# Query and key parts laid out feature by feature, with three gathers for each, in a two-layer adaLN transformer kernel

## What is computed

```python
h = layernorm(x) * (1 + ca) + sa                   # sa..gb from silu(c) @ wmod
x = x + ga * attention0(h)                         # linear attention, chunks of 64, RoPE, biases bq bk bv bg
x = x + gb * mlp0(layernorm(x) * (1 + cb) + sb)    # 256 -> 2048 -> 256, weights in 4-bit codes
x = x + ga1 * attention1(...)                      # causal softmax attention, RoPE, biases bq bk
x = x + gb1 * mlp1(...)                            # holds a second causal softmax attention, 1024 hidden
```

## Time and profile before

| | us |
|---|---|
| median of 3 runs | 713.77 |
| lowest and highest run | 713.38, 720.05 |
| the profiled execution's own time | 716.44 |
| its span, first to last instruction | 714.7 |
| mean granted TensorE clock | 0.976 |

### The profile page before, as it was taken

One profiled execution on the slowest core, in us unless ns is written; L12 is line 12 of the kernel. 1 busy time (PEld: TensorE's weight loads), 2 busy tenths in 40 slices (PEclk: granted clock), 3 DMA queues, 4 the chain that ended last, 5 costly groups with the idle time before them and its releaser, 6 DMA issues.

```text
span 714.7 us, 10679 instructions
## 1 busy us (share of the span) xinstructions
PE 651.3 (91%) x3977; PEld 409.9 (57%) x3977; DVE 463.9 (65%) x970; ACT 334.4 (47%) x531; POOL 164.6 (23%) x200
## 2 busy tenths in 40 slices
PE   3699988999999979799999998888999999989996
PEld 3576746777777747444444434574554444368885
DVE  5868776777777388688988801656689887243223
ACT  3335143333333333336567685561555657843332
POOL 6601133555555431210000000030000001002231
PEclk9999599999999999899999999997999999999999
DMA  9502320000000001573000000037420000050001
GB/s 319 164 1 89 89 82 0 23 22 23 1 0 1 0 1 44 182 218 91 3 2 1 2 2 1 0 98 223 134 81 2 2 2 3 1 176 1 0 1 59
DMA packets 36335, 38.35 MB, mean 54 GB/s; under 512 B 3958, under 2 KB 35204, under 8 KB 36028
## 3 DMA queue, kind: packets, MB, share of 16 engines
q1 hardware_dynamic: 36284, 37.68, 16.7%
HBM read 30.13 MB, written 7.34 MB: 52 GB/s over the span
## 4 chain that ended last, share of the span: by engine, by line
PE 47%; issue 22%; POOL 12%; DVE 11%; ACT 3%; DMA 2%; SPq 2%; POOLq 0%; DVEq 0%; ACTq 0%
POOL it_lo L1601 9%; PE psum L777 9%; PE psum L737 8%; PE psum L763 8%; PE psum L452 3%; PE psum L454 3%; PE psum L453 3%; POOL wd L1580 2%; PE psum L495 2%; PE psum L566 2%; SPq L408 2%; PE psum L766 2%; PE psum L740 2%; DVE m L1280 2%; DVE stats L1103 1%
## 5 line engine op out<-in xcount | busy, mean ns | idle before, releaser
L957 ACT ACTIVATE pt<-psum 128x1024 f32<-128x1024 f32 (+1 forms) x192 | 148.0, 811 | 92.9 <-PE psum L766 64.7
L1280 DVE TENSOR_REDUCE mx<-psum 128x1 f32<-128x512 f32 (+3 forms) x216 | 132.4, 665 | 16.3 <-PE psum L737 8.3
L737 PE MATMUL psum<-kr,qr 96*128 96x512 bf16 (+3 forms) x384 | 111.0, 341 | 5.4 <-DMA kr<-parts_scratch 2.5
L1601 POOL TENSOR_TENSOR it_lo<-it,it_hi 128x512 fp32r<-128x512 f32 x48 | 67.3, 1401 | 153.6 <-ACT it_hi L1001 153.6
L763 PE MATMUL psum<-qr,kr 99*128 99x512 bf16 (+3 forms) x384 | 97.6, 327 | 1.5 <-ACT pt L957 1.3
L777 PE MATMUL psum<-pt,vp 128*32 128x512 f32 (+3 forms) x768 | 81.7, 498 | 0.0
L452 PE MATMUL psum<-h_hi,wf_hi 128*128 128x512 f32 x192 | 75.5, 393 | 1.7 <-issue 1.7
L737 PEld LDWEIGHTS psum<-kr,qr 96*128 96x128 bf16 x384 | 37.1, 100 | 67.5 <-DVE mx L1280 29.4
L453 PE MATMUL psum<-h_lo,wf_hi 128*128 128x512 f32 x192 | 75.0, 390 | 0.0
L454 PE MATMUL psum<-h_hi,wf_lo 128*128 128x512 f32 x192 | 74.9, 390 | 0.0
L1001 ACT CAST it_hi<-it 128x512 fp32r<-128x512 f32 x48 | 29.8, 622 | 95.7 <-DVE it L1355 95.7
(11 more groups left out here) (204 smaller groups left out, 1111.2 us busy)
## 6 DMA issues: line engine op xcount, KB each, us to landing
qr<-parts_scratch SPq DMA_DIRECT2D x48, 128.0 KB, 2.7
kr<-parts_scratch SPq DMA_DIRECT2D x48, 128.0 KB, 2.6
parts_scratch<-parts SPq DMA_DIRECT2D x12, 384.0 KB, 3.5
wmod<-in_L_wmod SPq DMA_DIRECT2D x1, 1536.0 KB, 6.1
parts_scratch<-qr SPq DMA_DIRECT2D x4, 384.0 KB, 3.3
x<-in_L_attn_x SPq DMA_DIRECT2D x2, 512.0 KB, 4.0
wmod<-in_L_wmod SPq DMA_DIRECT2D x1, 1024.0 KB, 7.2
packed<-in_L_ffn_gate_W_packed SPq DMA_DIRECT2D x1, 1024.0 KB, 9.2
```

The lines of the kernel that those rows point to most:

```text
L737: m = pe.matmul(b, qr[0:PARTS_ROWS, c, h, (qt - 4 * c) * P:(qt - 4 * c + 1) * P], kr[0:PARTS_ROWS, ch, h, 0:w], start=True, stop=not diag)
L957: act.activation(pt[:, n % 4, :, 0:w], psum[:, b:b + 2, 0:w], ACT.Exp, scale=0.25).then_inc(S["ex"], 1)
L1280: dve.tensor_reduce(dst, bank[at[0]][:, 0:k * w].rearrange("p (k w) -> p k w", k=k), AX, ALU.max).then_inc(S["p1_mx"], 1)
L1601: pool.tensor_tensor(it_lo[:, N % 2, :], it[:, N % 2, :], it_hi[:, N % 2, :].bitcast(F32), ALU.subtract).then_inc(S["it_l"], 1)
```

## The change

- `scr` is laid out [piece, half, part, feature, token]. The columns of the four q and k weight matrices of the second block, and bq and bk of its first attention, are reordered on the way in, so that 16 features x 8 heads follow each other as feature, head; RoPE (`pairs`, `rope_cos`, `rope_sin`) uses views for this order when l = 1 (the first softmax attention; here l counts the block).
- `spread` issues 3 gathers for q and 3 for k, into 48, 32 and 16 neighbouring partitions, each row 8 heads x 512 tokens. For k the source is the first 3, 2, 1 parts, as they lie in scratch. For q it is one part, repeated 3, 2, 1 times by a step of zero. The writes of q and k have semaphores of their own, and the gathers of q wait only for that of q.
- `rest` has four buffers. The overlay of `qr`/`kr` over the mlp's tiles is reordered so that the memset of the -1 rows is split in four behind the last four `it_lo` of mlp(0).
- Biases are loaded once as 12 partitions x 128, split there by POOL in four operations, and brought to 3 partitions x 1536 by three DMAs; SP waits for POOL before it issues these, and issues them ahead of the rest of `wmod0` and what follows. `spin` takes the place of `sel`.
- `idle(14, 0)` is `idle(5, 0)`, `idle(4, 3)` is gone, and ACT computes the Silu ahead of the square root.

```diff
@@ -219,7 +219,7 @@
         y = xn[:, :, :].rearrange("p a b -> p (a b)").rearrange("p (c t) -> p c t", c=KC)
-        rest = xn[:, 0:4, :].rearrange("p a b -> p (a b)").rearrange("p (c t) -> p c t", c=2)
+        rest = xn[:, :, :].rearrange("p a b -> p (a b)").rearrange("p (c t) -> p c t", c=4)
         att = xn
@@ -240,15 +240,16 @@
-        ((packed, wf_hi, wf_lo, wd, nib, sgn, dbl, r16, gl, it, it_hi, it_lo), (_, v1, g, qT, cum, km), (nat,),
+        ((wf_hi, wf_lo, gl, it, it_hi, it_lo, packed, wd, nib, sgn, dbl, r16), (v1, g, qT, km, _, _, cum), (_, nat),
-            [("packed", [P, 3 * F0], I32), ("wf_hi", [P, 2, 6 * P], F32R), ("wf_lo", [P, 2, 6 * P], F32R),
-             ("wd", [P, 2, 6 * P], F32), ("nib", [P, 6 * P], U16), ("sgn", [P, 6 * P], U16),
-             ("dbl", [P, 6 * P], BF16), ("r16", [P, 4 * P], U16), ("gl", [P, 2, HALF], F32),
-             ("it", [P, 2, HALF], F32), ("it_hi", [P, 2, HALF], F32R), ("it_lo", [P, 2, HALF], F32R)],
-            [("packed_", [P, 3 * F0], I32), ("v1", [P, NT, 2, VW], F32), ("g", [P, NT, D], F32),
-             ("qT", [P, KC, T], F32), ("cum", [P, 4, 2, VW], F32), ("km", [P, 2, 2, VW], F32)],
-            [("nat", [P, 3 * F0], F32)],
+            [("wf_hi", [P, 2, 6 * P], F32R), ("wf_lo", [P, 2, 6 * P], F32R), ("gl", [P, 2, HALF], F32),
+             ("it", [P, 2, HALF], F32), ("it_hi", [P, 2, HALF], F32R), ("it_lo", [P, 2, HALF], F32R),
+             ("packed", [P, 3 * F0], I32), ("wd", [P, 2, 6 * P], F32), ("nib", [P, 6 * P], U16),
+             ("sgn", [P, 6 * P], U16), ("dbl", [P, 6 * P], BF16), ("r16", [P, 4 * P], U16)],
+            [("v1", [P, NT, 2, VW], F32), ("g", [P, NT, D], F32), ("qT", [P, KC, T], F32),
+             ("km", [P, 2, 2, VW], F32), ("gap", [P, 7168 - 2 * NT * VW - NT * D - KC * T - 4 * VW], F32),
+             ("packed_", [P, 3 * F0], I32), ("cum", [P, 4, 2, VW], F32)],
+            [("gap2", [P, 7168], F32), ("nat", [P, 3 * F0], F32)],
@@ -269,8 +270,9 @@
-        bias = sb("bias", [P, 6 * D], BF16)
-        sel = sb("sel", [P, P], BF16)
+        brow = sb("brow", [12, P])
+        bpart = sb("bpart", [12, 3, P], BF16)
+        bias = sb("bias", [3, 6 * D], BF16)
@@ -311,22 +313,23 @@
-        scr = nc.dram_tensor("parts_scratch", [4, P, 3, T], BF16, kind="Internal").ap()
+        scr = nc.dram_tensor("parts_scratch", [4, NH, 3, P, HALF], BF16, kind="Internal").ap()
-            idz sel_ok bias_z bias_s bias_ok ident_ok spin_ok const_ok vp_ones kr_ones a_rep_ok b_zero
+            idz bias_s bias_ok ident_ok spin_ok const_ok vp_ones kr_ones a_rep_ok b_zero
+        names += [f"{z}w{i}" for z in "qk" for i in range(4)]
@@ -350,14 +353,16 @@
+            load(brow[:, :], a["bias_rows"].rearrange("(c p) -> c p", p=P), "ld_bias")
             wm0 = a["L0_wmod"].rearrange("(c p) n -> p c n", p=P)
                 load(raw0[:, i], a[f"L0_attn_W{n}"].rearrange("(o p) k -> p o k", p=P), "ld_raw0")
-            sp.wait_ge(S["bias_z"], 1)
-            load(rb[0:P:32, 0:4 * D], a["bias_rows"][0:4 * D].partition_broadcast(4), "ld_bias")
             load(rope_c[:, :, :, :], a["rope_cos"].rearrange("p (l t d) -> p l t d", l=2, t=NT), "ld_rope")
             load(rope_s[:, :, :, :], a["rope_sin"].rearrange("p (l t d) -> p l t d", l=2, t=NT), "ld_rope")
+            sp.wait_ge(S["bias_s"], 4)
+            for i in range(3):
+                load(bias[i:i + 1, :], bpart[:, i, :], "bias_ok")
             load(wmod0[:, :, 512:1536], wm0[:, :, 512:1536], "ld_wmod0b")
@@ -366,8 +371,6 @@
             load(a_nat[:, :, :], a["L1_ffn_A"].rearrange("(o p) r -> p o r", p=P), "ld_a")
-            sp.wait_ge(S["bias_ok"], 1)
-            load(rb[0:P:32, 0:2 * D], a["bias_rows"][4 * D:6 * D].partition_broadcast(4), "ld_bias")
             sp.wait_ge(S["b_zero"], 1)
@@ -394,20 +397,21 @@
                     w2 = 2 * dt + is_k
-                    tok = slice(half * HALF, (half + 1) * HALF)
                     sp.wait_ge(*low_part(l, 4 * half + w2))
-                    sp.dma_start(scr[w2, :, :, tok], piece(l, w2, half)).then_inc(S[f"pw{2 * half + dt}"], 16)
+                    sp.dma_start(scr[w2, half].rearrange("s p t -> p s t"), piece(l, w2, half)).then_inc(S[f"{'qk'[is_k]}w{2 * half + dt}"], 16)
-
-                tok = slice(half * HALF, (half + 1) * HALF)
-                sp.wait_ge(S[f"pw{2 * half + dt}"], 32 * (l + 1))
-                for is_k, (dst, order) in enumerate([(qr, (0, 1, 0, 1, 0, 2)), (kr, (1, 1, 2, 2, 0, 1))]):
-                    for slot, part in enumerate(order):
-                        sp.dma_start(dst[slot:PARTS_ROWS:6, half, 8 * dt:8 * dt + 8, :],
-                                     scr[2 * dt + is_k, :, part, tok].rearrange("(h d) t -> d h t", d=DH)
-                                     ).then_inc(S[f"qr_ld{2 * half + dt}"], 16)
+                for is_k, dst in enumerate((qr, kr)):
+                    sp.wait_ge(S[f"{'qk'[is_k]}w{2 * half + dt}"], 16 * (l + 1))
+                    for part, (first, n) in enumerate(((0, 3), (3, 2), (5, 1))):
+                        src = scr[2 * dt + is_k, half].rearrange("s (d h) t -> s d (h t)", d=DH)
+                        if is_k:
+                            src = src[0:n]
+                        else:
+                            src = src[part:part + 1].to_broadcast([n, DH, 8 * HALF])
+                        sp.dma_start(dst[DH * first:DH * (first + n), half, 8 * dt:8 * dt + 8, :].rearrange("r h t -> r (h t)"),
+                                     src).then_inc(S[f"qr_ld{2 * half + dt}"], 16)
@@ -474,8 +478,10 @@
                 if b0 is not None:
-                    pe.wait_ge(S["bias_ok"], 1 + b0 // T)
-                    m = pe.matmul(dst, sel[:, :], bias[:, b0:b0 + c1 - c0], start=False, stop=True)
+                    if b0 == 0 and t == 0:
+                        pe.wait_ge(S["spin_ok"], 1)
+                        pe.wait_ge(S["bias_ok"], 48)
+                    m = pe.matmul(dst, spin[0:3, 0:P], bias[:, b0:b0 + c1 - c0], start=False, stop=True)
                 return m
@@ -632,7 +638,7 @@
             pe.wait_ge(S["spin_ok"], 1)
-            idle(14, 0)
+            idle(5, 0)
             pe.wait_ge(S["const_ok"], 1)
@@ -720,15 +726,13 @@
-                if l == 0:
-                    idle(4, 3)
                 loaded = []
                             loaded.append((g // 2, c))
-                            pe.wait_ge(S[f"qr_ld{2 * c + g // 2}"], 16 * 12 * (l + 1))
+                            pe.wait_ge(S[f"qr_ld{2 * c + g // 2}"], 16 * 6 * (l + 1))
                         bank_free(at[1])
@@ -753,7 +757,7 @@
                                 idle(6, 4)
-                                pe.wait_ge(S["kr_ones"], 1)
+                                pe.wait_ge(S["kr_ones"], 4)
                             nb = len(BLOCKS) * l + blk
...
@@ -919,7 +923,7 @@
-                    act.copy(piece(l, n, half)[:, (1, 2)[n % 2], :], rest[:, w % 2, :]
+                    act.copy(piece(l, n, half)[:, (1, 2)[n % 2], :], rest[:, w % 4, :]
...
@@ -1005,8 +1011,8 @@
             act.wait_ge(S["vec_ok"], 1)
+            act.activation(silc[:, :, :], vec[:, 0:2, :], ACT.Silu).then_inc(S["silu_c"], 1)
             layer_norm_std(0)
-            act.activation(silc[:, :, :], vec[:, 0:2, :], ACT.Silu).then_inc(S["silu_c"], 1)
             for i in range(4):
@@ -1169,16 +1175,19 @@
-                return ap.rearrange("p (h two j) -> p h two j", h=2 * H, two=2)[:, :, i, :]
+                return ap.rearrange("p (g two j h) -> p g two j h", g=4, two=2, h=8)[:, :, i, :, :]
-                dve.tensor_tensor(t1[:, t % 2, :].rearrange("p (h d) -> p h d", d=DH),
-                                  bank[4 + 2 * (t % 2)][:, :].rearrange("p (h d) -> p h d", d=DH),
-                                  rope_c[:, l, t, :].unsqueeze(1).to_broadcast([P, 2 * H, DH]), ALU.mult
-                                  ).then_inc(S["rp_t1"], 1)
+                if l == 0:
+                    z = [v.rearrange("p (h d) -> p h d", d=DH) for v in (t1[:, t % 2, :], bank[4 + 2 * (t % 2)][:, :])]
+                    c = rope_c[:, l, t, :].unsqueeze(1).to_broadcast([P, 2 * H, DH])
+                else:
+                    z = [v.rearrange("p (g d h) -> p g d h", g=4, h=8) for v in (t1[:, t % 2, :], bank[4 + 2 * (t % 2)][:, :])]
+                    c = rope_c[:, l, t, :].unsqueeze(1).unsqueeze(3).to_broadcast([P, 4, DH, 8])
+                dve.tensor_tensor(z[0], z[1], c, ALU.mult).then_inc(S["rp_t1"], 1)
@@ -1187,7 +1196,11 @@
-                    q = dve.tensor_tensor(z[0], z[1], s.unsqueeze(1).to_broadcast([P, 2 * H, DH // 2]), ALU.mult)
+                    if l == 0:
+                        s = s.unsqueeze(1).to_broadcast([P, 2 * H, DH // 2])
+                    else:
+                        s = s.unsqueeze(1).unsqueeze(3).to_broadcast([P, 4, DH // 2, 8])
+                    q = dve.tensor_tensor(z[0], z[1], s, ALU.mult)
@@ -1213,15 +1226,15 @@
-                        if w >= 2:
```

(64 more changed lines are left out.)

15 lines of the change are left out of this document (9 added, 6 removed).

## The result

The changed kernel takes 765.0 us (four runs, 760.7 to 770.2) against 713.6 for the kernel before: a ratio of 1.069, with a 95% interval of 1.064 to 1.074. I had forecast 727, in a range of 711 to 741. It is slower by the mechanism named, but by 51 us where I had 13. Some executions of a kernel run at a lower granted clock and take longer; the ratios leave them out, the medians do not.

A forecast was written before the change was run, and what follows sets the result against it. PE, busy 91% of the span, was taken to bound the kernel, with attention starts hanging on transfers. 716.4 - 7.1 - 0.2 - 0.6 + 8 + 8 + 5 = 729.5 us profiled, median 727, range 711 to 741.

The forecast's parts named there:

- The first stage: Before the projections: Silu ahead of the square root and POOL's smaller bias split let DVE finish earlier; gain 7.1 us.
- third rival: Attention gathers: k's are as narrow as q's, a quarter takes 20.7 us, median 778 us; chance 0.07.
- each us of a quarter moves the end by six: Both attentions: each us of a quarter's time on the busiest DMA engine moves the kernel's end by six us.
- 39 rows of 8 KB: 39 x 0.314 = 12.2 us: Attention gathers: engine 0 moves 33 rows of q and 6 of k per quarter, in 12.2 us.
- forecast 16: Both attentions: the first score of block 1 comes later behind the narrow gathers, 8 us lost in each.
- forecast 5 for the clock: Both attentions: PE's new wait before block 1 brings a lower granted clock, costing 2.5 us each, 5 in all.
- The bias product keeps its 512 columns.: First stage: the bias product's column count is unchanged; no cost was counted for it.
- The idle products: Ahead of the first output product: nine idle products fewer gain 0.2 us, with 0 and 2.0 as ends.
- the -1 rows: Memset of the -1 rows, split in four behind POOL's last low parts: gain 0.6 us.
- the views of RoPE: RoPE on DVE: same elements and instructions, so 0, with 0.1 us for each of 24 instructions as a bound.
- All gathers are wide: Attention gathers: all use sixteen engines and SP's halved issues save time; 704.0 us, median 701; chance 0.11.
- Partly hidden: Attentions: PE waits at block 1 but later work catches up, half of the 16 us lost; median 714; chance 0.09.

The follow-up runs named there:

- the run with POOL busy: The changed kernel with POOL also doing the old bias split's four operations, on a tile of zeros, in the first stage: 773.9 us, ratio 1.081.
- the one with other partitions: The changed kernel with part 0's copies at partitions 48 to 95, part 1's at 0 to 31, part 2's at 32 to 47: 754.7 us, ratio 1.052.
- the copies inside: The changed kernel with gathers running over a part's 16 rows first, copies of q and parts of k inside each: 708.9 us, ratio 0.991.
- the two runs with q alone: The changed kernel with SP waiting for q's gathers before issuing k's: 792.9 us; the same with part 0 at partitions 48 to 95, part 1 at 0 to 31: 763.4.
- The variants with wide gathers: The changed kernel with gathers on sixteen engines: copies inside 708.9 us, also into every second partition 708.8; twelve gathers into every sixth 707.8, plus 128-row bias product 704.0 and 703.1.

## Why the prediction was wrong

**What held.** The q gathers use three and two engines, the k gathers sixteen. Everything behind them on those engines waits. The first stage came as worked out (7.3 for 7.1), and the run with POOL busy shows the reason to be right. The first score of block 1 waits for its row maximum, and k is wide (third rival out). That each us of a quarter moves the end by six held where the order of SP's work stayed: 5.7 to 6.8 between the changed kernel and the one with other partitions, 6.6 (56.1 / 8.5) between it and the copies inside. Where SP itself waits for q, each us costs more: 29.6 us for 3.2 between the two runs with q alone.

**The step that failed: "39 rows of 8 KB: 39 x 0.314 = 12.2 us".** The count is right: in the DMA records of the changed kernel a chain of 39 rows of 8 KB, each starting where another ends, runs from 279.47 to 297.49. The time of a row is not: these are 18.0 us, 0.46 for a row. 0.314 came from a transfer over the whole tile in the earlier trace rows, whose engines are spread over all partitions. It is the time of an undisturbed row (0.309 in the tails above), and I used it for all. Three things make the narrow gathers slower. Two of the three engines write partitions 32 apart and take 0.62 a row, as the two runs with q alone show (16.6 against 13.8). K's rows, on all sixteen engines and into neighbouring partitions, slow most rows to 0.4 to 0.9 for some 5 us; 166 GB/s at a share of 0.95 is that. And some of each engine's first rows take 0.8 to 1.1 us. Together a quarter took 20.2 instead of 14.6.

How the 5.6 divide depends on the order in which the causes are taken away. The slow first rows are 1.1: with q alone in the other places 33 rows take 11.44 us, where 33 x 0.314 is 10.36. The partitions 32 apart are 2.8 with q alone, 1.8 with k beside. K's six rows of the busiest engine should add 1.9; they add 3.6 (16.6 to 20.2), and in the other places 4.6 (13.8 to 18.4), so that the slowing beside k is 1.7 or 2.7. 1.1 + 2.8 + 1.7 and 1.1 + 1.8 + 2.7 are both 5.6.

No row of before gave the right number. The row-max transfer in the earlier trace rows is at 45 / (0.20 x 16) = 14 GB/s for each engine, and 8 KB at that rate would take 0.58 us, which is near. But the trace has that transfer in pieces of 256 bytes at 18 ns each, so the nearness is chance. What could have been done is to carry a range for the rate: the bounds of the count (12 to 66 rows) were stated, those of the rate only as 23 GB/s in place of 26.1.

**Where the 48.3 us of the span came from.** Up to the first write of q and k: 5.25 gained, forecast 7.9. From there to the first score of block 1, in both attentions together: 22.3 + 22.8 = 45.1 lost, forecast 16. Behind these scores 5.0 and 3.4, together 8.4 lost, forecast 5 for the clock. So 29.1 of the 35.2 us between the forecast and the profiled execution (729.5 and 764.7) are the failed step, a little under its own six times 5.6 = 34.

**The term left out: "The bias product keeps its 512 columns."** True, and beside the point. Its contraction went from 128 rows to 3, and that costs 0.30 us each time, which turns the 7.3 us gained at the start into 2.4. The end shows 5 to 6. Without it the start would have gained about 10 us (5.25 + 4.8, an estimate), more than the forecast's 7.9. The Trainium skill, "TensorEngine Tiling (Array Packing)", section "Key Properties", says that changing the tiling mode drains TensorE. The product behind the bias product starts 0.32 us after it, against 0.04 with 128 rows. That would agree with such a cost, but no run here shows that the mode changes or separates it from the number of rows.

**The other terms.** The idle products, the -1 rows and the views of RoPE are too small to be told apart here. The clock falls in the waits (0.63 and 0.50 from 290 to 298), and the first score of block 1 takes 0.61 us where it took 0.38; how much of the 8.4 us behind the scores is the clock, no run shows.

**The rivals.** "All gathers are wide" was forecast at 701 for a kernel with wide gathers. The variants with wide gathers gave 708 and 709, and 703 to 704 once the bias product was mended. "Partly hidden" is out: PE's waits came in full and more.
